# Delta rule: the convolution's taps as fused multiply-adds on VectorE, and the queries' read-out scaled per head on ScalarE

## The reference, cut to what matters

```python
mixed_qkv = _causal_conv_silu(hidden_states @ W_qkv, conv_w)   # silu(sum of 4 shifted taps), per channel
q = _l2norm(q) * DK ** (-0.5)
k = _l2norm(k)
def step(S, xs):
    q_t, k_t, v_t, g_t, b_t = xs
    S = S * jnp.exp(g_t)[..., None, None]
    kv = jnp.einsum('bhk,bhkv->bhv', k_t, S)
    S = S + jnp.einsum('bhk,bhv->bhkv', k_t, (v_t - kv) * b_t[..., None])
    o_t = jnp.einsum('bhk,bhkv->bhv', q_t, S)
    return (S, o_t)
...
o = o * jax.lax.rsqrt(var + EPS) * norm_w * jax.nn.silu(z)
return o.reshape(b_, t_, V_DIM) @ W_out
```

## Time and profile before

| what | value |
|---|---|
| time, median of 3 runs | 2650.12 us (2644.24 to 2650.3) |
| profiled execution: its time, its span | 2650.15 us, 2648.4 us |
| PE, DVE, ACT, POOL busy, share of the span | 80%, 70%, 54%, 30% |
| PE, DVE, ACT, POOL busy in 1160 to 2030 us (870 us) | 766.69, 783.63, 584.10, 396.50 us |
| instructions in the span | 63269 |

### The profile page before, as it was taken

One profiled execution on the slowest core, in us unless ns is written; L12 is line 12 of the kernel. 1 busy time (PEld: TensorE's weight loads), 2 busy tenths in 40 slices (PEclk: granted clock), 3 DMA queues, 4 the chain that ended last, 5 costly groups with the idle time before them and its releaser, 6 DMA issues. The chain is left out here.

```text
span 2648.4 us, 63269 instructions
## 1 busy us (share of the span) xinstructions
PE 2112.3 (80%) x25432; PEld 1309.6 (49%) x25432; DVE 1862.2 (70%) x4409; ACT 1441.6 (54%) x2941; POOL 799.0 (30%) x852
## 2 busy tenths in 40 slices
PE   2698988988888485479899888888888885677984
PEld 1244444444444264245556565555655553454652
DVE  2477777777776335688999989899998983672333
ACT  0366677677676223666666766766666543222221
POOL 1000001001001134124444444344444442104884
PEclk9599999999998797688988988998999987698997
DMA  5000000000000161100000000000000003234334
GB/s 186 37 1 1 9 5 9 5 5 9 5 5 9 33 173 47 28 10 11 13 12 12 13 12 12 13 12 12 8 8 14 5 4 97 73 109 97 44 45 88
DMA packets 109525, 85.51 MB, mean 32 GB/s; under 512 B 22366, under 2 KB 97282, under 8 KB 108976
## 3 DMA queue, kind: packets, MB, share of 16 engines
q1 hardware_dynamic: 95664, 68.31, 8.8%
q0 software_dynamic: 13568, 13.14, 3.1%
HBM read 59.22 MB, written 22.71 MB: 31 GB/s over the span
## 5 line engine op out<-in xcount | busy, mean ns | idle before, releaser
L624 ACT ACTIVATE Pr<-Pr,nmax 128x512 f32<-128x512 f32 x512 | 341.3, 714 | 173.0 <-DVE nmax L555 168.3
L729 PE MATMUL bank<-ident,Pr 128*128 128x128 f32 x2048 | 301.6, 289 | 82.5 <-DVE PT L564 64.6
L729 PEld LDWEIGHTS bank<-ident,Pr 128*128 128x128 f32 x2048 | 232.0, 147 | 254.9 <-DVE PT L564 163.4
L555 DVE CUSTOM_DVE_ANT_0 Pr<-bank,Tb 128x512 f32<-128x512 f32 x512 | 331.0, 684 | 22.9 <-PE bank L715 21.6
L564 DVE COPY PT<-bank 128x512 f32<-128x512 f32 x256 | 176.4, 689 | 176.1 <-PE bank L743 171.6
L2486 PE MATMUL bank<-Wcv,hw 128*128 128x512 f32 x512 | 261.1, 657 | 6.0 <-ACT bank L2275 5.1
L2101 DVE TENSOR_TENSOR pr<-AC,Tc 128x30 f32<-128x30 f32 (+14 forms) x480 | 212.2, 442 | 20.2 <-POOL Tc L1969 6.3
L2102 DVE TENSOR_TENSOR Tc<-Tc,pr 128x30 f32<-128x30 f32 (+14 forms) x480 | 187.6, 391 | 16.5
L631 ACT ACTIVATE PT<-bank 128x512 f32<-128x512 f32 x256 | 150.9, 590 | 71.8 <-PE bank L743 66.9
L715 PE MATMUL bank<-kp,qp 8*128 8x512 f32 x1024 | 172.5, 663 | 0.8 <-DVE nmax L555 0.8
L1918 POOL TENSOR_TENSOR Xs<-vt,Xs 128x512 f32<-128x512 f32 x64 | 80.3, 1273 | 285.4 <-DVE Xs L2011 285.3
(11 more groups left out here) (409 smaller groups left out, 4362.2 us busy)
## 6 DMA issues: line engine op xcount, KB each, us to landing
aB<-alpha SPq DMA_DIRECT2D x64, 128.0 KB, 2.8
Tb<-scores SPq DMA_DIRECT2D x1, 7168.0 KB
w<-in_L_ffn_W SPq DMA_DIRECT2D x16, 256.0 KB, 5.4
rawW<-in_L_ffn_up_w SPq DMA_DIRECT2D x16, 256.0 KB, 3.1
rawW<-in_L_ffn_gw SPq DMA_DIRECT2D x16, 256.0 KB, 3.5
rawW<-in_L_ffn_down_w SPq DMA_DIRECT2D x16, 256.0 KB, 4.3
disp<-zero SPq DMA_DIRECT2D x1, 2580.0 KB, 15.2
xin<-disp SPq DMA_DIRECT2D x8, 322.5 KB, 6.3
```

The costliest lines, as they stand in the source:

```text
L555: V.tensor_tensor_reduce(out=Pr[:, s, i, :], in0=pS[hh][:, :], in1=Tb[:, h, at:at + L], scale=-1.0, scalar=3.0e38, op0=ALU.add, op1=ALU.mi ...
L624: A_(Pr[:, s, i, :], Pr[:, s, i, :], ACT.Exp, scale=-1.0, bias=nmax[:, s, i:i + 1])\
L729: last = TR(pT[m % 2][:, t * P:(t + 1) * P], Pr[:, (G % 2) * HG + hh, t, j * P:(j + 1) * P], ident[:, :])
```

## The change

Three edits. VectorE's `conv` no longer adds three prepared taps but multiplies and adds `raw` itself: six `scalar_tensor_tensor` instructions of 256 columns, the tap a per-partition scalar read from `cw`, in three pairs, with a wait between pairs; `yp` and ScalarE's six tap instructions per call are gone, and `conv` waits for ScalarE's `a_m` in place of `a_yp`. The scaling of the queries' read-out leaves VectorE's `read_out`; ScalarE does it in `decayed`, eight copies of 64 columns for each half, placed behind the second `square_out`; who waited for `v_qs` (VectorE `accumulate`, TensorE `attend`) waits for `a_qs`. GpSimd's `halo` waits for `v_conv` in place of `a_yp`.

```diff
--- before.py
+++ after.py
@@ -1772,15 +1772,14 @@
     HF = HV // 2
     Wqk, Wcv, Wz, Wo, cw, hT, bT, gT, GC = [w[n] for n in ("Wqk", "Wcv", "Wz", "Wo", "cw", "hT", "bT", "gT", "GC")]
     with Stage(nc, ["p_ks", "p_qs", "p_w", "p_ds", "p_pu", "p_kk", "p_m",
-                    "v_ks", "v_qs", "v_s", "v_o", "v_lt", "v_at", "v_ac", "v_tt", "v_conv", "v_ss",
+                    "v_ks", "a_qs", "v_s", "v_o", "v_lt", "v_at", "v_ac", "v_tt", "v_conv", "v_by", "v_ss",
                     "v_rn", "v_rk", "p_nm", "p_nt", "a_rt", "v_sr", "v_link", "g_x", "g_s", "g_d1", "g_t", "g_t0", "g_halo", "g_on", "g_hw", "g_ac", "v_nm", "a_kq", "g_ud",
-                    "a_m", "a_w", "a_yp", "a_on", "a_sq", "a_osq", "a_or", "a_lk", "d_al0", "d_al1", "d_out",
+                    "a_m", "a_w", "a_on", "a_sq", "a_osq", "a_or", "d_al0", "d_al1", "d_out",
                     "k_y0", "k_y1", "k_y2", "k_y3", "k_m", "k_x", "k_v", "k_var", "k_rstd", "k_nm", "k_xn", "k_xT", "k_hT",
                     "k_rows", "k_be", "k_e", "k_ee", "k_al", "k_alz", "k_ad", "k_ga", "k_gb", "k_gce"]) as s:
         raw = s.sb("raw", [P, 4, 2, 4, KS - 1 + 2 * CK])
         hw = s.sb("hw", [P, 2, KS, 4, CK])
         yc = s.sb("yc", [P, 2, 2, 4, 2 * CK])
-        yp = s.sb("yp", [P, KS - 1, 2, 4, 2 * CK])
         sq = s.sb("sqc", [P, 2, 2, 2, 2, P])
         rkq = s.sb("rkq", [P, 3, 2, 2, HK])
         rq2 = s.sb("rq2", [P, 2, HK])
@@ -1950,7 +1949,7 @@
                     m, tp = t // 4 + 1, t % 4
                     if m == NP:
                         return
-                    pool.wait_ge(s["a_yp"], t + 1)
+                    pool.wait_ge(s["v_conv"], t + 1)
                     if m % (NP // 2) == 0:
                         G.memset(raw[:, tp, :, :, 0:KS - 1], 0.0).then_inc(s["g_halo"], 1)
                     else:
@@ -2011,11 +2010,6 @@
                     V.tensor_tensor(hd(Xs[:, f, :]), hd(BK[f][:, :]),
                                     bcast(gk[:, k // 2 % 2, k % 2, HF * f:HF * f + HF], 2, DK), ALU.mult)\
                         .then_inc(s["v_ks"], 1)
-                    dve.wait_ge(s["p_qs"], half(k, f))
-                    if k >= 2:
-                        dve.wait_ge(s["p_m"], done("ot", 2 * (k - 2) + f))
-                    V.tensor_tensor(hd(O[:, k % 2, f, :]), hd(BQ[f][:, :]), cols(gT, k, f), ALU.mult)\
-                        .then_inc(s["v_qs"], 1)
 
                 def squares(k, f):
                     if k >= 2 and f == 0:
@@ -2060,14 +2054,21 @@
                     V.transpose(rkT[:, :], rkd[:, :, :].rearrange("p e h -> p (e h)"))
 
                 def conv(t):
-                    dve.wait_ge(s["a_yp"], t + 1)
-                    flat = lambda x: x.rearrange("p j x t -> p (j x t)")
-                    link(V.tensor_tensor(BY[:, :], BY[:, :], flat(yp[:, 2, :, :, :]), ALU.add))
-                    link(V.tensor_tensor(BY[:, :], BY[:, :], flat(yp[:, 1, :, :, :]), ALU.add))
-                    if t >= 2:
-                        dve.wait_ge(s["a_kq"], t - 1)
-                    V.tensor_tensor(flat(yc[:, t % 2, :, :, :]), BY[:, :], flat(yp[:, 0, :, :, :]), ALU.add)\
-                        .then_inc(s["v_conv"], 1)
+                    tp = t % 4
+                    dve.wait_ge(s["a_m"], done("pj", t))
+                    for i in (2, 1, 0):
+                        if i == 0 and t >= 2:
+                            dve.wait_ge(s["a_kq"], t - 1)
+                        for j in range(2):
+                            acc = BY[:, 256 * j:256 * j + 256].rearrange("p (x t) -> p x t", x=4)
+                            last = V.scalar_tensor_tensor(acc if i else yc[:, t % 2, j, :, :],
+                                                          raw[:, tp, j, :, i:i + 2 * CK],
+                                                          cw[:, TILE[2 * tp + j], i:i + 1], acc, ALU.mult, ALU.add)
+                            if i:
+                                last.then_inc(s["v_by"], 1)
+                        if i:
+                            dve.wait_ge(s["v_by"], 4 * t + 2 * (3 - i))
+                    last.then_inc(s["v_conv"], 1)
 
                 def attend(c):
                     m, e = c // 2, c % 2
@@ -2119,7 +2120,7 @@
 
                 def accumulate(k, f):
                     dve.wait_ge(s["p_pu"], half(k, f))
-                    dve.wait_ge(s["v_qs"], half(k, f))
+                    dve.wait_ge(s["a_qs"], half(k, f))
                     V.tensor_tensor(O[:, k % 2, f, :], O[:, k % 2, f, :], BQ[f][:, :], ALU.subtract)\
                         .then_inc(s["v_o"], 1)
 
@@ -2252,6 +2253,16 @@
                         act.wait_ge(s["v_sr"], half(k, f) - 1)
                     A_(osq[:, :], O[:, k % 2, f, :], ACT.Square).then_inc(s["a_osq"], 1)
 
+                def decayed(k, f):
+                    act.wait_ge(s["p_qs"], half(k, f))
+                    if k >= 2:
+                        act.wait_ge(s["p_m"], done("ot", 2 * (k - 2) + f))
+                    for h in range(HF):
+                        of = slice(DK * h, DK * h + DK)
+                        at = k // NCK * HV + HF * f + h
+                        last = A_(O[:, k % 2, f, of], BQ[f][:, of], ACT.Copy, scale=gT[:, k % NCK, at:at + 1])
+                    last.then_inc(s["a_qs"], 1)
+
                 def root(m):
                     act.wait_ge(s["p_nm"], m + 1)
                     A_(roots, BKK[0:2 * HK, 0:2 * P].rearrange("p (e t) -> p e t", e=2), ACT.Sqrt,
@@ -2267,19 +2278,14 @@
                     act.wait_ge(s["p_m"], done("pj", t))
                     act.wait_ge(s["g_halo"], t + 1)
                     bank = M[USE[("pj", t)] % 2][:, :].rearrange("p (j x t) -> p j x t", j=2, x=4)
-                    A_(raw[:, tp, :, :, KS - 1:KS - 1 + 2 * CK], bank, ACT.Copy).then_inc(s["a_lk"], 1)
+                    A_(raw[:, tp, :, :, KS - 1:KS - 1 + 2 * CK], bank, ACT.Copy)
                     if t:
                         act.wait_ge(s["v_conv"], t)
-                    tap = lambda j, i: cw[:, TILE[2 * tp + j], i:i + 1]
+                    tap = lambda j: cw[:, TILE[2 * tp + j], KS - 1:KS]
                     for j in range(2):
                         last = A_(BY[:, 256 * j:256 * j + 256].rearrange("p (x t) -> p x t", x=4), bank[:, j, :, :],
-                                  ACT.Copy, scale=tap(j, KS - 1))
+                                  ACT.Copy, scale=tap(j))
                     last.then_inc(s["a_m"], 1)
-                    act.wait_ge(s["a_lk"], t + 1)
-                    for i in (2, 1, 0):
-                        for j in range(2):
-                            last = A_(yp[:, i, j, :, :], raw[:, tp, j, :, i:i + 2 * CK], ACT.Copy, scale=tap(j, i))
-                    last.then_inc(s["a_yp"], 1)
 
                 def squash(t):
                     act.wait_ge(s["v_conv"], t + 1)
@@ -2392,6 +2398,9 @@
                         output(k - 2)
                     if past:
                         square_out(k - 1, 1)
+                    if here:
+                        decayed(k, 0)
+                        decayed(k, 1)
                     if here and k % 2 == 1:
                         weights(k, 0)
                     if (k + 4) // 2 < NP:
@@ -2565,7 +2574,7 @@
 
                 def attend(k, f):
                     pe.wait_ge(s["a_w"], half(k, f))
-                    pe.wait_ge(s["v_qs"], half(k, f))
+                    pe.wait_ge(s["a_qs"], half(k, f))
                     if f == 0:
                         pe.wait_ge(s["v_at"], k + 1)
                     for h in range(HF):
```

## The result

| kernel | median | runs | ratio to before, 95% interval |
|---|---|---|---|
| before, on the same chip | 2649.09 us | 2644.24 to 2650.3 | |
| the change | 2628.79 us | 2624.6 to 2636.14 | 0.9931 [0.9916, 0.9946] |

Slower by 37 us was forecast (2687); the change is faster. By the ratio it gains 18 us. The medians differ by 20, because the median before counts one execution of 3964.72 us that neither the range nor the ratio does. The profiled execution took 2624.6 us (span 2622.8), 25.5 less than the one before.

A forecast was written before the change was run, and what follows sets the result against it. VectorE, 90% busy, was taken to bound the loop, tied by the lock to GpSimd's chain. 14 x (0.8 + 1.7) = 35.0 us and 1.5 made 36.5 on 2650.15: 2687 us; case range 2660 to 2702, overall 2640 to 2712.

The forecast's parts named there:

- The convolution's price: VectorE's fused convolution: 2.65 us a call against 2.06, so 0.59 us more, the SBUF scalar costing 0.06 an instruction.
- locked scalar: Rival: fused convolution instructions are held by running GpSimd instructions; 28 us more, 2715 us; chance 0.12.
- Read-out at nothing: Taking 1.20 us a step of read-out off VectorE gains nothing in each of the 32 steps.
- busy time rules: Rival: what leaves the 90% busy VectorE is won; 2646 us, or 2624 with 0.20 a call; chance 0.16.
- the lock: VectorE instructions with inputs in SBUF that meet a running GpSimd instruction stand until it ends; those with a bank operand don't.
- Even step +0.8: Even steps: both convolution calls pay, 1.18 us, less 0.4 for a vanishing wait on TensorE's product before `A`: 0.8 more.
- Odd step +1.7: Odd steps: second convolution 0.59 us, GpSimd's `Ud` and S product meeting `substitute` net 1.3, less 0.2 for waits: 1.7 more.
- Waits on TensorE worth nothing: VectorE's 33.0 us of waits at `update`, mostly in even steps: if they shrink, the 5.41 us stretch stays.
- TensorE's wait: Rival: `Ws` comes earlier in even steps too, and the 33.0 us at `update` fall away; 2619 us; chance 0.12.
- Prelude and end: Eight calls before the loop: nothing net; the last step's copies ahead of `Ws`: 1.5 us more, from 0 to 3.9.

The follow-up runs named there:

- e1: Against the kernel before: only the queries' read-out scaling moved to ScalarE, convolution left as it was; 2642.59 us, ratio 0.9979.
- e2: Against the kernel before: only the fused convolution, read-out scaling kept on VectorE; 2693.06 us, ratio 1.0163.
- e5: e2 with GpSimd's second `Ud` in odd steps also waiting for the first instruction pair of VectorE's second convolution; 2654.04 us, ratio 1.0023.
- e3: The change with ScalarE's six tap instructions put back, writing a buffer nobody reads, and GpSimd's halo copy waiting for them; 2657.88 us, ratio 1.004.
- e8: The kernel before with `norms` (`bk`, `gk`, `rkd` of even steps) issued ahead of `squares` and `read_out`; 2639.15 us, ratio 0.9966.
- e4: The change with a constant in place of the tap scalar read from SBUF, so it computes something else; 2635.22 us, ratio 0.9948.
- e7: The change with `norms` (`bk`, `gk`, `rkd` of even steps) issued ahead of `squares` and `read_out`; 2632.52 us, ratio 0.9944.
- e9: The change with GpSimd's second residual in even steps waiting until VectorE has made `bk`, `gk`, `rkd`; 2630.49 us, ratio 0.994.
- e10: e1 with GpSimd's second residual in even steps waiting until VectorE has made `bk`, `gk`, `rkd`; 2624.85 us, ratio 0.9924.
- e13: The kernel before with GpSimd's second residual in even steps waiting until VectorE has made `bk`, `gk`, `rkd`; 2632.9 us, ratio 0.9936.

## Why the prediction was wrong

Taken by its own steps:

- **The convolution's price**, 2.65 us a call, 0.59 more: right. That it passes beside GpSimd untouched, scalar and all: right (the second call above lies on GpSimd's `Ud` and S product), so the "locked scalar" rival falls.
- **Read-out at nothing**: nearly right where it stands alone (e1 gains 6.2 us in the 26 steps, of 31 taken from VectorE), wrong in company. "Started 1.2 us sooner they end at the same point" assumes that GpSimd's instructions stay where they were against the first `Xs`. With both parts VectorE got ahead of TensorE, the second `Xs` of an even step and the first `Ws` of an odd one waited for it, and in the gaps on GpSimd the small products passed. The rival "busy time rules" named that point, that "the small products escape the lock when they come 1.2 us earlier"; it had 0.16.
- **Even step +0.8**: right for the long kind (36.0 us against 35.1 for the undisturbed ones before), but eight of 13 were of the short kind, 0.8 below. Measured in the mean -0.4; this step made 16 of the 44 us between forecast and measured in the 26 steps.
- **Odd step +1.7: the term that failed**, with 28 of the 44 us. It put the second `Ws` 1.5 us earlier and the start of `substitute` at 6.3 us, unchanged. For that it let the first `Ws` follow ScalarE's copies, at 4.0 to 4.7 us, and left TensorE's place in the step as it was. In the change's step 7 the copies ended at 4.1, but `Ws` waited for TensorE to 5.4; the second `Ws` came 0.85 earlier and `substitute` at 5.3, so the S product missed it. The stretch was 0.8 instead of 2.3, and 1.0 was gained at `nrm`; measured -0.4 in the mean. Step 7 was also taken for every odd step: before, `substitute` started at 6.3 in eight of the 12 with an S product there, and at 5.5 in four. The mechanism is real: with the convolution alone (e2) the second `Ws` is at 9.9 us, the S product meets `substitute`, and a step costs 3.1 more; a wait removes it (e5). It wasn't met in the change.
- **Waits on TensorE worth nothing**: half right. The 5.41 us from the end of `turn` stood (17.2 to 22.6 in the short step). But e3 brought 25.3 us of waits back and 29 us with them; the rival "TensorE's wait", at 2619, came nearer than the other two by their main figures, and in e8 that wait took back some 6 us. e3 doesn't part the two, since its even steps went over to the long kind as well: six steps more, at 1.7 us each, would be 10 of the 25 us by which its 26 steps are longer.
- **Prelude and end**: -0.7 against 0, and +1.4 from the start of step 28 to the stage's last instruction against +1.5: right.
- **Not in the prediction: TensorE's clock.** Over the 26 steps the granted clock is 0.92 before and 0.94 in the change. The change's odd steps of 31.0 us have 1.00, those of 31.8 have 0.95; in e2, e4, e7 and e9 the odd steps of 34 us and more have 0.85 or 0.86, all of them with a stretch of 4.2 us or more in which TensorE was idle. No run changes the clock alone, so how much of the 11.3 us it carries, and how much of the waits at `update`, stays open.
- **Not in the prediction: steps 0 and 1**, 7.2 us shorter in the profile. The windows view over TensorE's read-out of step 0, before and then in the change (the granted clock is the column before the last two):

```profile
1154.07:1160.29 6.22, 6.22 (x130) 5.35 (x129) 3.47 (x5) 3.71 (x9) 2.14 (x2) 0.50 0.01 3
```

```profile
1147.43:1150.74 3.31, 3.31 (x130) 3.11 (x129) 2.85 (x5) 2.60 (x10) 1.16 (x1) 1.00 0.02 5
```

It ran at 1.2 GHz before and at 2.4 in the change, shortly after 2.80 us of idle time against 1.37. All 16 profiles split this way: eight have 2.8 us of idle time there, a read-out of 5.8 to 6.2 us at a clock of 0.50 to 0.55, and 71 to 74 us for the two steps; eight have 1.1 to 1.4 us, 3.31 us at 1.00, and 63 to 66. e2 and e5 have the same instructions up to there and are of different forms, so it can differ between executions. The five kernels with plain sums in every convolution (before, e1, e8, e10, e13) had the slow form, eight of the 11 others the fast one. So the change may make the fast form likelier; whether it does stays open.

## What to carry over

Where VectorE and GpSimd hold each other up, a part's worth isn't a property of the part: the same two edits gave -5.5 and +45 us alone and -18 together. So work out each step's start on both engines with every rival's shift before summing, and above all ask which third engine (here TensorE) becomes the last one when both run ahead. Then place the collisions by hand: a wait on a semaphore that moves GpSimd's instruction off VectorE's small SBUF instructions, onto those that work in PSUM, gave 7 to 37 us in six kernels here by the ratios, and nothing in a seventh, where it left another collision open. And look at a collision's price on the third engine as well: in e2 it made TensorE idle, its clock fell, and VectorE waited another 1.4 us for it.

## What was unexpected in the hardware

- VectorE's fused instruction that reads one input and its scalar from SBUF and accumulates in a bank runs in 0.48 us beside GpSimd's products (146 of them in the change) as away from them (161); with a constant scalar (e4) it is 0.42; small instructions of 0.18 us with SBUF inputs become 0.9 to 1.9. The Trainium skill (SBUF — State Buffer, Who interferes with whom) counts SBUF inputs; by that rule this one, with a single such input, is free, and the trace agrees and adds that the scalar's place doesn't count.
- Not every VectorE instruction that reads SBUF is held, as the prediction's sentence on the lock would have it: the reduction of `osq` (L2024, 128x512) took 0.67 us in the 16 places before where it ran wholly beside a GpSimd product, and 0.67 away from one.
- The collision costs GpSimd something too: beside `substitute` its `Ud` took 1.23 and its S product 2.06 us in e2, 1.04 and 1.90 in e5 where they lie beside the convolution.
